# Router rounds in another order, weights split through PSUM, smaller transfers around the first expert mixture

## The reference, cut to what matters

```
x = x + attn0(layernorm(x))                 # o, centred and normalised, gated, times Wout
xn = layernorm(x)
logits = relu(xn @ rw1 + rb1) @ rw2 + rb2   # 8 experts, best 2 of each token
disp[expert, pos] = xn                      # pos: running count, at most 512 per expert
eo = relu(disp @ ew1 + eb1) @ ew2 + eb2     # per expert
x = x + sum over 2 picks of eo[expert, pos] * prob * keep
x = x + attn1(layernorm(x)); x = x + mixture1(layernorm(x))
```

## Time and profile before

| | us |
|---|---|
| median of 3 runs | 928.38 (927.70 to 929.48) |
| the profiled execution | 927.65 |
| its span in the profile | 925.6 |
| stage 5, begin to end | about 208.3 to 323.0 |
| first transposes of stage 6 | 329.48 |
| first fetch queued, first `combine` | 388.47, 392.40 |

### The profile page before, as it was taken

The page is one execution under the profiler, slowest core; times in us unless marked ns, Lnnn a source line. Parts: engine busy times, 40 slices in busy tenths (PEclk is TensorE's granted clock), DMA queues, the critical chain, the costliest instruction groups (busy, mean ns, idle before and its releaser), DMA issues.

```text
span 925.6 us, 18384 instructions
## 1 busy us (share of the span) xinstructions
PE 774.7 (84%) x6154; PEld 469.3 (51%) x6154; DVE 693.2 (75%) x2078; ACT 622.2 (67%) x932; POOL 632.3 (68%) x414
## 2 busy tenths in 40 slices
PE   4965765669998689468787989999999999999997
PEld 1343221224543357323233756767776777777775
DVE  7769899985777558498999878776666666666664
ACT  3755233323455367248778988888888888989895
POOL 4008899730577727558798997686868686868695
PEclk9987899899999899879999999999999999999999
DMA  5999300008200030252600000000000000000000
GB/s 150 118 120 202 115 0 0 18 3 211 69 21 7 3 101 26 68 149 58 204 1 1 1 1 2 13 1 11 0 11 0 8 4 0 11 0 11 0 13 13
DMA packets 52761, 40.47 MB, mean 44 GB/s; under 512 B 6028, under 2 KB 44703, under 8 KB 52703
## 3 DMA queue, kind: packets, MB, share of 16 engines
q1 hardware_dynamic: 49630, 37.28, 18.5%
q0 software_dynamic: 3072, 2.51, 0.9%
HBM read 18.07 MB, written 14.88 MB: 36 GB/s over the span
## 4 chain that ended last, share of the span: by engine, by line
POOL 24%; PE 18%; issue 14%; DVE 14%; ACT 6%; DMA 1%; POOLq 0%; DVEq 0%; ACTq 0%; SPq 0%
POOL scratch L725 20%; PE PS L1874 17%; DVE scratch L1635 2%; DVE resid L1537 2%; DVE stats L1375 1%; DVE scratch L1643 1%; POOL disp L635 1%; POOL resid L711 1%; PE PS L1881 1%; ACT scratch L1163 1%; ACT scratch L1159 1%; DVE resid L1388 1%; DVE A L1400 1%; DVE scratch L1378 1%; ACT A L1094 1%
## 5 line engine op out<-in xcount | busy, mean ns | idle before, releaser
L725 POOL TENSOR_TENSOR scratch<-scratch 128x1024 f16<-128x1024 f32 x128 | 273.0, 2135 | 84.5 <-ACT scratch L1163 82.3
L1822 DVE SCALAR_TENSOR_TENSOR resid<-PS,coef,resid 128x128 f32<-128x128 f32 x512 | 144.0, 344 | 108.8 <-PE PS L1874 103.4
L1874 PEld LDWEIGHTS PS<-A,scratch 128*128 128x128 f16 x3456 | 203.4, 98 | 37.9 <-POOL scratch L725 4.9
L1874 PE MATMUL PS<-A,scratch 128*128 128x128 f16 x3456 | 217.1, 219 | 3.9 <-POOL scratch L725 1.6
L1874 PE MATMUL PS<-A 128*128 (+1 forms) x768 | 186.8, 379 | 0.8 <-DVE A L1666 0.2
L1159 ACT ACTIVATE scratch<-PS,cols 128x512 f32<-128x512 f32 x256 | 163.9, 683 | 25.9 <-PE PS L1874 19.0
L1163 ACT ACTIVATE scratch<-scratch 128x1024 f16<-128x1024 f32 x128 | 135.3, 1057 | 5.0
L1874 PE MATMUL PS<-scratch,ident 128*128 128x512 f32 x160 | 89.4, 681 | 51.9 <-DVE scratch L1341 51.9
L594 POOL TENSOR_TENSOR scratch<-A 128x1024 f32<-128x1024 f32 x32 | 76.0, 2384 | 73.2 <-DVE A L1310 56.2
L1874 PEld LDWEIGHTS PS<-A 128*128 128x128 f16 x768 | 70.7, 98 | 66.6 <-issue 0.7
L635 POOL DMA_INDIRECT disp<-A,scratch x64 | 65.5, 1023 | 36.4 <-issue 30.0
(11 more groups left out here) (334 smaller groups left out, 1321.0 us busy)
## 6 DMA issues: line engine op xcount, KB each, us to landing
A<-A SPq DMA_DIRECT2D x22, 256.0 KB, 7.5
y_rows<-zeros SPq DMA_DIRECT2D x8, 512.0 KB, 6.0
A<-y_rows SPq DMA_DIRECT2D x16, 256.0 KB, 3.5
disp<-zeros SPq DMA_DIRECT2D x4, 528.0 KB, 21.6
A<-disp SPq DMA_DIRECT2D x4, 528.0 KB, 6.0
resid<-in_L_attn_x SPq DMA_DIRECT2D x8, 256.0 KB, 4.0
A<-scratch SPq DMA_DIRECT2D x8, 256.0 KB, 6.9
A<-in_L_ffn_ew SPq DMA_DIRECT2D x1, 2048.0 KB, 12.4
```

Source lines behind the costliest of these rows:

```text
L725: pool.tensor_tensor(h_low[n % 4], h_full[n % 2], h_high[n % 4], SUB).then_inc(S("m1_low"), 1)
L1822: last = STT(out=resid[:, g, :], in0=bank(4 + e % 2)[:, t * C:(t + 1) * C], scalar=coef[b % 2][:, t, e:e + 1], in1=resid[:, g, :], op0=MUL ...
L1874: return nc.tensor.matmul(o, l, r, start=start, stop=stop)
```

## The change

TensorE's round becomes: first half of `router_hidden(b)`, `count_picks(b-1)`, `variance_o(b+1)`, `project0(b+1)`, second half of `router_hidden(b)`, `router_logits_T(b)`, `transpose5(b+1)`, `router_logits(b)`, `centre(b+2)`. So the variance and the projection of a batch stand one round later, and the centring behind the logits. ScalarE and VectorE are put in matching orders. Three weight splits' high parts are made in rounds 5 to 7. For six splits ScalarE also copies the high part, as f32, into PSUM (`weights0_beside`), and VectorE's low split reads it from there. The copy of the output biases (`eb2_rep`) moves behind the splits. In the first batch of scatters the wait for the next logits stands before the seventh transfer, not the fifth. `xd` is loaded in parts of 1, 1, 3 and 3 experts. The first fetch of `y_rows` is cut into four transfers of half a batch, and the later fetches wait for one batch less. In stage 6 the hidden layer of expert 7 stands between the two halves of the outputs of expert 6.

```diff
+        EARLY, BESIDE = 3, 6
+        def high_at(k):
+            return bank(k % 2 * 2, 2)
+        XD_PARTS = ((0, 1), (1, 2), (2, 5), (5, E0))
...
-            for k in range(E0 // 2):
-                sp.dma_start(xd[:, bts(k, 2 * NT), :], dv[:, bts(k, 2 * NT), :]).then_inc(s_disp[k], 16)
+            for k, (low, high) in enumerate(XD_PARTS):
+                part = slice(low * NT, high * NT)
+                sp.dma_start(xd[:, part, :], dv[:, part, :]).then_inc(s_disp[k], 16)
...
+                if b == 0:
+                    for half in range(2):
+                        for k in range(TOP0):
+                            part = slice(half * NT // 2, (half + 1) * NT // 2)
+                            sp.dma_start(fetched[k][:, part, :], yv[k][:, part, :]).then_inc(s_disp[half], 16)
+                    continue
...
-                    if t == NT // 2 and b + 1 < B:
+                    if t == (NT // 2 if b else NT - 1) and b + 1 < B:
                         pool.wait_ge(S("lg5_mm"), at(b + 1))
...
 # ScalarE
+            def weights0_beside(k):
+                hl = (e0_hl1, e0_hl2)[k // 4]
+                if k >= 2:
+                    act.wait_ge(S("split_low"), at(E0_SPLITS + k - 2))
+                act.wait_ge(S("split_high"), high_made(k))
+                A_(high_at(k), hl[:, 2 * (k % 4):2 * (k % 4) + 2, 0, :], ACT.Copy).then_inc(S("split_high"), 1)
+
+            for b in range(B):
+                for h in range(HC0):
+                    relu5(b, h)
+                    if h == 1 and b >= 1 and b + 1 < B:
+                        deviation_o(b + 1)
+                if b + 1 < B:
+                    deviation_x5(b + 1)
+                lgT5_copy(b)
+                if b + 1 < B:
+                    xT5_copy(b + 1)
+                if b + 2 < B:
+                    square_o(b + 2)
+                if b >= B - EARLY:
+                    act.wait_ge(s_wm, 32)
+                    act.wait_ge(s_scattered[0], 16 * TOP0 * NT * 4)
+                    weights0_high(b - B + EARLY)
+            for k in range(EARLY):
+                weights0_beside(k)
             act.wait_ge(S("lg_less"), at(0))
             A_(tmpb[:, :], tmpa[:, :], ACT.Exp).then_inc(S("lg_exp"), 1)
...
-            for k in range(6):
+            for k in range(EARLY, BESIDE):
                 weights0_high(k)
+                weights0_beside(k)
...
 # VectorE
-                if b and b + 2 < B:
-                    gate_o(b + 2)
                 if b and b + 1 < B:
                     xT5_low(b + 1)
                 route(b, b % 2)
                 if b == 0:
                     xT5_low(1)
+                if b and b + 2 < B:
+                    gate_o(b + 2)
                 place_picks(b, b % 2)
...
-            dve.wait_ge(s_eb2_mm, 1)
-            st.done(V.tensor_copy(eb2_rep, bank(6, 2).rearrange("p k (e c) -> p (k e) c", c=C)))
...
-                dve.wait_ge(S("split_high"), at(E0_SPLITS + k))
-                STT(out=hl[:, two, 1, :], in0=w[:, two, :], scalar=SCALE, in1=hl[:, two, 0, :],
+                dve.wait_ge(S("split_high"), beside_made(k) if k < BESIDE else high_made(k))
+                STT(out=hl[:, two, 1, :], in0=w[:, two, :], scalar=SCALE, in1=high_at(k) if k < BESIDE else hl[:, two, 0, :],
                     op0=MUL, op1=SUB).then_inc(S("split_low"), 1)
...
+            for k in range(BESIDE):
                 weights0_low(k)
+            dve.wait_ge(s_eb2_mm, 1)
+            st.done(V.tensor_copy(eb2_rep, bank(6, 2).rearrange("p k (e c) -> p (k e) c", c=C)))
...
 # TensorE
                 router_hidden(b, range(HC0 // 2))
-                if b == 1:
-                    variance_o(2)
-                elif b:
+                if b >= 2:
                     count_picks(b - 1, (b - 1) % 2)
+                if b >= 1 and b + 1 < B:
+                    variance_o(b + 1)
+                    project0(b + 1)
                 router_hidden(b, range(HC0 // 2, HC0))
-                if b == 1:
-                    project0(2)
-                if b and b + 2 < B:
-                    centre(b + 2)
                 router_logits_T(b)
                 if b + 1 < B:
                     transpose5(b + 1)
-                if b and b + 2 < B:
-                    variance_o(b + 2)
                 router_logits(b)
+                if b + 2 < B:
+                    centre(b + 2)
...
+                if e == E0 - 2:
+                    outputs0(e, range(NT // 2))
+                    hidden0(e + 1)
+                    outputs0(e, range(NT // 2, NT))
+                    continue
```

More of the change, by code:

```diff
@@ L383, in build, with high_made, beside_made @@
         E0_SPLITS = 2
+        EARLY, BESIDE = 3, 6
+        def high_made(k):
+            return at(E0_SPLITS + (k if k < EARLY else 2 * k if k < BESIDE else k + BESIDE))
+        def beside_made(k):
+            return at(E0_SPLITS + (EARLY + k if k < EARLY else 2 * k + 1))
+        def high_at(k):
+            return bank(k % 2 * 2, 2)
         PARTS = ((0, 0), (0, 1), (1, 0))
+        XD_PARTS = ((0, 1), (1, 2), (2, 5), (5, E0))
+        XD_PART_OF = (0, 1, 2, 2, 2, 3, 3, 3)
         r7 = carve(7)[:, 688:688 + 2 * TILES].rearrange("p (s n) -> p s n", s=2)
@@ L503, in _ @@
             for b in range(B):
-                if b >= 2:
-                    sp.wait_ge(s_fetched[b % 2], X_LOADS + 16 * TOP0 * (b // 2))
+                if b == 0:
[4 more added lines that the diff above has]
+                    continue
+                if b >= 3:
+                    sp.wait_ge(s_fetched[b % 2], X_LOADS + 16 * TOP0 * ((b - 1) // 2))
                 for k in range(TOP0):
@@ L628, in scatter @@
                 for t in range(NT):
-                    if t == NT // 2 and b + 1 < B:
+                    if t == (NT // 2 if b else NT - 1) and b + 1 < B:
                         pool.wait_ge(S("lg5_mm"), at(b + 1))
-                    elif t == NT // 2:
+                    elif t == NT // 2 and b + 1 == B:
                         pool.wait_ge(s_eb2_mm, 1)
@@ L890, in weights0_high @@
                 A_(hl[:, two, 0, :], w[:, two, :], ACT.Copy, scale=SCALE).then_inc(S("split_high"), 1)
+            def weights0_beside(k):
[22 more added lines that the diff above has]
+                weights0_beside(k)
             act.wait_ge(S("lg_less"), at(0))
             A_(tmpb[:, :], tmpa[:, :], ACT.Exp).then_inc(S("lg_exp"), 1)
-            act.wait_ge(s_wm, 32)
-            act.wait_ge(s_scattered[0], 16 * TOP0 * NT * 4)
             act.wait_ge(s_scattered[1], 16 * TOP0 * NT * (B - 5))
-            for k in range(6):
+            for k in range(EARLY, BESIDE):
                 weights0_high(k)
+                weights0_beside(k)
             stage_end(act, 5)
@@ L1532, in combine @@
             def combine(b):
[L1533 to L1540, removed]
+                if b:
+                    dve.wait_ge(s_fetched[b % 2], X_LOADS + 16 * TOP0 * ((b + 1) // 2))
+                for part in ((0, 1), (2, 3)) if b == 0 else (range(NT),):
+                    if b == 0:
+                        dve.wait_ge(s_disp[part[0] // 2], BACK[part[0] // 2] + 16 + 16 * TOP0)
+                    for k in range(TOP0):
+                        for t in part:
+                            g = b * NT + t
+                            last = STT(out=resid[:, g, :], in0=fetched[k][:, g, :], scalar=coef0[:, k, g:g + 1],
+                                       in1=resid[:, g, :], op0=MUL, op1=ADD)
+                        if k < TOP0 - 1:
+                            links.done(last)
                 last.then_inc(S("moe_added"), 1)
@@ L1591, in gates_low @@
                 TT(gate_hl[:, 1, c], whole_gate(m), gate_hl[:, 0, c], SUB).then_inc(S("gate_low"), 1)
-            dve.wait_ge(S("split_high"), at(E0_SPLITS + 8))
+            dve.wait_ge(S("split_high"), high_made(8))
             for low, w, high in ((u1_hl[:, 1, :], u_1[:, :], u1_hl[:, 0, :]), (u2_hl[1], u_2[:, :, :], u2_hl[0]),
@@ L2054, in _ @@
                     transpose5(b + 1)
-                if b and b + 2 < B:
-                    variance_o(b + 2)
                 router_logits(b)
+                if b + 2 < B:
+                    centre(b + 2)
                 if b == 0:
-                    centre(2)
                     unread(3, 4)
                     count_picks(0, 0)
-                elif b + 2 < B:
-                    project0(b + 2)
             count_picks(B - 1, 1)
@@ L2069, in _ @@
             last.then_inc(s_eb2_mm, 1)
-            unread(3, 20)
+            unread(4, 20)
             stage_end(pe, 5)
@@ L2075, in transpose_rows @@
             def transpose_rows(e):
-                pe.wait_ge(s_disp[e // 2], BACK[e // 2] + 16)
+                pe.wait_ge(s_disp[XD_PART_OF[e]], BACK[XD_PART_OF[e]] + 16)
                 pe.wait_ge(S("xdT"), at(e, 2))
@@ L2088, in hidden0, with outputs0 @@
                     last.then_inc(S("m0_hid_mm"), 1)
-            def outputs0(e):
+            def outputs0(e, tiles=range(NT)):
```

(2 more changed lines are left out.)

## The result

The changed kernel takes 938.0 us (median of 4 runs, 937.43 to 938.3) against 928.93 us (4 runs of the kernel before on the same chip): a ratio of 1.0103, interval 1.009 to 1.0115, about 9.1 us slower. Forecast was 938.6. The profiled execution took 937.85 us with a span of 935.7, 10.1 us over the span before.

A forecast was written before the change was run, and what follows sets the result against it. TensorE, with next to no idle time in router rounds, was taken as the bound. Start of stage 6 +8.3, experts 6 and 7 +2.9, fetch -0.6 made +10.6: 938.3, forecast as 938.6 us, range 932.5 to 941.5.

The forecast's parts named there:

- step-by-step list: Router round timed from ScalarE's copy of the logits (t): 12.16 instead of 10.51 us, +8.4 over all rounds.
- low bound: Router rounds: if only the relu wait is exposed, a round is 11.34 us, +4.4 in all.
- The scatters' gain: Stage 5: first batch gains 2.56 us, lost because later batches wait for longer rounds; scatters run at 0.97 throughout.
- The splits: End of stage 5: VectorE's tail behind the last round takes 14.3 instead of 13.6 us, 0.7 longer.
- The dummies: Behind stage 5: 18 dummies take 5.64 us, end at 337.8 and set the start of stage 6.
- rival D: Router rounds: TensorE's idle time lowers its granted clock, +2.6 a round, 950 or more; chance 0.03.
- Experts 6 and 7: End of stage 6: outputs(6) wait for `m0_low`, hidden(7) and the last scatters come later, +2.9 us.
- Rival A: Stage 6: the reordering brings first outputs to GpSimd sooner, -1.0 instead of +2.9, 934.4; chance 0.10.
- The fetch: Behind stage 6: halving the first fetch lets the first adds start sooner, -0.6 us, bounds 0 and -2.0.
- B: Start of stage 6: the scatter chain still sets it and is freed, -6.0, total 924.0; chance 0.07.
- C: Router rounds stay at 10.5 us because some counted wait is covered, 930.0; chance 0.06.

The follow-up runs named there:

- x1: The changed kernel with the old order of the router rounds on TensorE, ScalarE and VectorE, early splits kept: 931.92 us, ratio 1.0046 to the kernel before.
- x10: The changed kernel with the variance of b+1 in front of the count of picks: 935.26 us, ratio 1.008 to the kernel before.
- x3: The changed kernel with only the centring of batch b+2 back in front of the logits: 936.93 us, ratio 1.0103 to the kernel before.
- y1: The kernel before, unaltered, run once more for a second profile: 927.57 us, ratio 1.0.
- x6: The kernel before with only the new order of experts 6 and 7, on a slower chip: 955.7 us, ratio 1.0044.
- x7: The kernel before with only the first fetch in four transfers and one fetch more in flight, on a slower chip: 949.66 us, ratio 0.9987.
- x2: The changed kernel with experts 6 and 7 in the old order: 934.42 us, ratio 1.0075 to the kernel before.
- y2: The changed kernel, unaltered, run once more for a second profile: 937.46 us, ratio 1.01 to the kernel before.
- y3: The changed kernel with old rounds, old order of experts and 6 instead of 18 dummies behind stage 5: 924.51 us, ratio 0.9958 to the kernel before.
- x11: y3 with ScalarE's exponential ahead of the third early copy into PSUM: 922.92 us, ratio 0.9949 to the kernel before.
- x8: The changed kernel with old rounds and old order of experts, on a slower chip: 947.71 us, ratio 0.9969 to the kernel before.
- x9: x8 with 6 instead of 18 dummies behind stage 5: 944.68 us, ratio 0.9934 to the kernel before.

## Why the prediction was right

**The round, right in mechanism and size.** Every start of my step-by-step list was met within 0.16 us: first half t + 1.97 (1.98), count 3.98 (4.02), variance 4.20 (4.35), second half 6.07 (6.23), logits 8.36 (8.52). x1 ties the 7.8 us to the order of the rounds, x10 moves the pick gap alone. One account in it was wrong, though the steps were right: I had put 1.00 us a round to the missing cover of the relus, as if the centring's place caused it, and my low bound (+4.4) stood on that wait alone. x3 has the centring back in front: the logits are covered and the round is no shorter, 11.98 us, since 0.92 us then opens in front of the first half.

**The scatters' gain, lost as said.** The first batch runs six scatters on end and its seventh waits 0.85 us, where the fifth had waited 3.93; but later batches wait for the logits of longer rounds, as in this one:

```profile
244.75 0.97 POOL L655 DMA_INDIRECT disp<-A,scratch  x1 [0.85 <-PE PS L2058]
...
280.75 0.97 POOL L655 DMA_INDIRECT disp<-A,scratch  x1 [2.07 <-PE PS L2058]
```

Beside the splits the scatters took 0.97 to 1.00 us where three had been slowed: what all of them lost over 0.97 sums to 0.4 us instead of 3.3. y1, x6 and x7, whose lows take both inputs from SBUF, have three or four slowed ones again, up to 1.97 us; in all profiles with the lows from PSUM, with new rounds or old, none behind T is over 1.04. No run changed the operand's place alone, so the shifted timing of the splits is not ruled out as the cause. By the Trainium skill (SBUF — State Buffer, "Who interferes with whom") a VectorE instruction with at most one SBUF input, outside its 2-port modes, doesn't contend with GpSimd. The trace agrees.

**The splits, right.** T to the stage's end grew by 0.50 (+0.7), with the table load bare and lows 2.1 us apart (2.07).

**The dummies, the term that I mis-sized.** I carried their 5.64 us over as a constant. They took 4.06 in the changed kernel, at a granted clock of 1.00; before, the clock was 0.50 for the first 3.2 us of them. In x1 they took 5.6, and TensorE had idled 4.18 us before them as against 2.95. The shorter idle time comes from the 20 dummies ahead, which took 7.28 us instead of 5.81 and ended later: the clock was 0.50 from 317.8 to 328.0. My rival D looked for a lower clock in the rounds only, and the sum had no term for it here. The start of stage 6 came 100.20 us behind the first scatter (236.29 to 336.49), where the sum has 102.7 (235.06 to 337.8). Of these 2.5 us the rounds are 0.6, the tail 0.2, and this one term 1.7.

**Experts 6 and 7, right.** +2.92 against +2.9. x2 shows it on the changed kernel, x6 the direction on the kernel before. Rival A fell with it: `m0_low` is late, as the row of VectorE said.

**The fetch, right in sign, too small.** -1.25 in the changed kernel, -0.7 from y1 to y2 and -0.9 by x7, against -0.6.

**What I had at zero.** 1.23 us upstream of stage 5 and 1.42 in the scans, both in code that no edit touches, make up for the dummies; so that 938.0 is so near to 938.6 is luck: the steps alone make +7.4 us, where I had +10.6. The 1.42 us go with the granted clock of the scans. The stretch behind the reciprocal is 528.9 and 529.0 in the two profiles before, at 1.00; 530.4 and 530.7 in the two after, at 0.94; x1, x2 and x10 have 0.94 and 530.9 to 531.0. But x3, which has the changed kernel's code behind the rounds, has 1.00 and 528.5:

```profile
440.00:530.00 90.00, 72.07 (x309) 33.90 (x308) 83.29 (x98) 75.45 (x105) 75.51 (x48) 1.00 0.21 59
```

So the program's text behind the rounds does not decide it; nor does it on the slower chip, where x6 and x7 share the scans of the kernel before and have 0.94 and 1.00 (531.4 and 529.0 us). The 1.23 us ahead of stage 5 don't go with this clock: first scatters lie anywhere from 234.97 to 237.01 us, and that of x3, with 1.00 in the scans, at 237.01. Of the 9.1 to 9.9 us that the kernel lost, 7.4 to 8.1 are the change's own. Why the changed kernel's two profiles both had the lower clock and the later first scatter stays open.

**Rivals.** B did not come about. Undo the rounds and the experts' order and cut the dummies (y3, x11), and part of its terms appears: -4 us between first scatter and reciprocal, the loads queued 2.5 us earlier behind the first scatter (87.75 in y3, 90.27 in y1; B had 5.1 for both of its scatter terms) and 3.0 to 3.1 us instead of 4.05 from there to the transposes. C fell with the 12.00 us round. D fell: in the window of one round the clock stays 1.00,

```profile
267.28:279.28 12.00, 10.52 (x56) 4.75 (x54) 8.29 (x47) 5.53 (x11) 7.79 (x8) 1.00 0.05 12
```

with TensorE busy 10.52 of 12.00 us.

## What to carry to other kernels

Where one engine is the bound and its order is written out, walk the new order step by step with durations from the trace: ask of each filler which handover it covered, and expect that moving it opens that gap while it closes another. When a part gains nothing, look at what stands unconditionally between it and the next stage; here leaving out 12 dummies brought three microseconds more (x8, x9). Compare by stretches between marks, so that drift in untouched code isn't booked to the edit.

## What the runs showed of the hardware

- The same 18 dummies took 4.06 us in six profiles (after, y2, x2, x3, x10, x6), 5.59 to 5.69 in four (before, y1, x1, x8) and 6.93 in x7. Spread over the time, 4.06 is 226 ns a matmul. In the slower ones the first matmuls (eight, in x7 fourteen) are 0.43 us apart and the rest 0.22, and the clock is granted at 0.50 for the first part and at 1.00 for the rest. TensorE had idled 2.89 to 3.80 us before the fast ones and 3.85 to 4.66 before the slow. The fast one with the longest idle time is x6:

```profile
338.95 4.06 PE L1874 MATMUL PS<-pickg,ones 128*128 128x512 f16 x18 [3.80 <-DVEq L181]
```

- Ten profiles of code without an edit, the scans (all but x6 to x9), split into 1.00 and 0.94 to 0.96 of granted clock, 528.5 to 529.0 us against 529.7 to 531.0.
- One chip (x6 to x9) granted 0.89 to 0.92 between 240 and 300 us, where the others granted 1.00, and ran the kernel before in 951.87 us, 2.6% more. The clock isn't all of it: in x8 the window from 255 to 270 us has 1.00, and still TensorE waits 1.00 and 2.03 us for ScalarE where y3, with the same rounds, doesn't. The cause stays open. The row of x8:

```profile
240.00:300.00 60.00, 52.44 (x262) 25.36 (x261) 39.48 (x220) 25.95 (x49) 35.54 (x38) 0.92 0.06 18
```
